# A Perceiver-style block with a mixture of experts on one core: one shared stage of the FFN moved from the front to the back, router and ranks ahead in TensorE's order, and later loads for the second block

## What is computed

```python
x = x + xattn(layernorm(x), ctx, ctx, w_proj, b_proj)      # 16 heads, softmax over 2048 keys
x = x + gated_scan_layer(layernorm(x), ...)                # tanh / sigmoid, scan over 128 rows, residual
x = x + ffn(layernorm(x), ...)

def ffn(xt):                                               # 512 tokens, 8 experts, top 2, 2 shared halves
    scores = softmax(xt @ gate_w.T); idx = top_k(scores + gate_bias, 2); weights = scores at idx
    for e in range(8):
        y += gate_e[:, None] * ((silu(xt @ w1[e].T) * (xt @ w3[e].T)) @ w2[e].T)
    z = (silu(xt @ sw1.T) * (xt @ sw3.T)) @ sw2.T          # inner width 1024: two halves of 512
    return y + z
```

## Time and profile before

| | |
|---|---|
| time, median of 3 runs | 541.11 us (536.25 to 542.07) |
| profiled execution, its run | 539.15 us |
| its span | 537.4 us |
| TensorE busy | 473.2 us (88%) |
| VectorE busy | 399.5 us (74%) |
| ScalarE busy | 330.2 us (61%) |
| GpSimd busy | 294.3 us (55%) |
| moved by DMA | 133.94 MB, mean 249 GB/s |

### The profile page before, as it was taken

How to read it: one execution, slowest core, us unless ns; L and a number is a source line. 1 busy time by engine, 2 the same in 40 slices (tenths; PEclk the granted TensorE clock), 3 DMA queues, 4 the chain that set the end, 5 groups by cost and what they waited for, 6 DMA issues and landing times.

```text
span 537.4 us, 15768 instructions
## 1 busy us (share of the span) xinstructions
PE 473.2 (88%) x6731; PEld 331.4 (62%) x6731; DVE 399.5 (74%) x603; ACT 330.2 (61%) x360; POOL 294.3 (55%) x278
## 2 busy tenths in 40 slices
PE   0579999798999898999989946997999999999995
PEld 0136667565666676666766533843788788887642
DVE  2686777477677677878762798788679999999426
ACT  3255867477567668776563463556478898887320
POOL 2358899699699999899769420472001011010032
PEclk9999999899899999999999995999999999999999
DMA  7798997959878879976696740228999999997135
GB/s 251 164 286 250 262 265 207 273 115 256 246 219 226 198 230 254 265 199 174 166 396 272 283 149 7 79 106 311 414 347 387 417 419 416 417 418 329 40 84 171
DMA packets 48249, 133.94 MB, mean 249 GB/s; under 512 B 6450, under 2 KB 31282, under 8 KB 37426
## 3 DMA queue, kind: packets, MB, share of 16 engines
q1 hardware_dynamic: 44500, 120.88, 69.6%
q0 software_dynamic: 3680, 12.06, 6.1%
HBM read 96.74 MB, written 11.01 MB: 201 GB/s over the span
## 4 chain that ended last, share of the span: by engine, by line
PE 45%; DVE 34%; issue 8%; DMA 7%; POOL 3%; ACT 1%; SPq 1%; DVEq 0%; ACTq 0%; POOLq 0%
DVE mx L696 12%; DVE ws L770 9%; PE bank L979 9%; PE bank L1014 8%; PE bank L1023 7%; PE bank L999 6%; DMA wst<-in_ffw 3%; DVE rden L713 2%; POOL xs_rows L660 2%; PE bank L1137 2%; PE bank L1139 2%; PE bank L1138 2%; DMA kt<-in_keysT 1%; DVE hf L908 1%; DMA x_tok<-xs_rows 1%
## 5 line engine op out<-in xcount | busy, mean ns | idle before, releaser
L696 DVE TENSOR_REDUCE mx<-bank 128x1 f32<-128x512 f32 x256 | 163.0, 685 | 67.9 <-PE bank L979 67.1
L457 ACT ACTIVATE pt<-bank 128x1024 f32<-128x1024 f32 x128 | 126.0, 1023 | 70.1 <-PE bank L999 70.1
L614 POOL TENSOR_TENSOR ps<-pt 128x512 f32<-128x512 f32 x128 | 160.0, 1277 | 10.1 <-ACT pt L457 5.2
L770 DVE SCALAR_TENSOR_TENSOR ws<-wst,ws 128x2048 f16<-128x2048 f32 x51 | 116.3, 2301 | 3.8 <-ACT ws L501 3.8
L979 PE MATMUL bank<-kstk,q 96*128 96x512 f16 x256 | 96.2, 407 | 24.9 <-DVE mx L696 8.1
L501 ACT ACTIVATE ws<-wst 128x2048 f16<-128x2048 f32 x48 | 90.4, 1904 | 7.1 <-DMA wst<-in_ffw 6.8
L999 PEld LDWEIGHTS bank<-q,kstk 98*128 98x128 f16 x1024 | 68.9, 100 | 22.5 <-issue 4.8
L587 POOL TENSOR_TENSOR kl<-kt,kh 128x512 f16<-128x512 f32 x62 | 70.6, 1162 | 22.3 <-ACT kh L422 22.3
L999 PE MATMUL bank<-q,kstk 98*128 98x128 f16 x1024 | 81.0, 224 | 1.0 <-ACT pt L457 1.0
L1152 PE MATMUL bank<-xt,ws 128*128 128x128 f16 x480 | 81.2, 219 | 0.6 <-DVE hf L908 0.6
L1153 PE MATMUL bank<-xt,ws 128*128 128x128 f16 x480 | 81.2, 219 | 0.0
(11 more groups left out here) (161 smaller groups left out, 639.0 us busy)
## 6 DMA issues: line engine op xcount, KB each, us to landing
wst<-in_ffw SPq DMA_DIRECT2D x51, 1024.0 KB, 10.8
kt<-in_keysT SPq DMA_DIRECT2D x16, 1024.0 KB, 6.0
kstk<-kh SPq DMA_DIRECT2D x128, 128.0 KB, 3.4
v<-in_vals SPq DMA_DIRECT2D x16, 1024.0 KB, 9.2
kstk<-kl SPq DMA_DIRECT2D x64, 128.0 KB, 3.7
xs_rows<-biases SPq DMA_DIRECT2D x15, 256.0 KB, 3.0
x_tok<-xs_rows POOLq DMA_DIRECT2D x15, 256.0 KB, 8.7
ys_rows<-xn POOLq DMA_DIRECT2D x15, 256.0 KB, 6.8
```

The lines of the kernel that those rows point to most:

```text
L457: act.activation(pt[:, n % 4, :, :, :].rearrange("p j a t -> p (j a t)"), bank[:, 2 * (n % 2):2 * (n % 2) + 2, :].rearrange("p j n -> p (j ...
L614: pool.tensor_tensor(ps2[:, n % 4, :, :], pt[:, n % 4, 0, :, :], pt[:, n % 4, 1, :, :], ALU.add)\
L696: dve.tensor_reduce(mx[:, a, q:q + 1], bank[:, 4 + k % 2, :], AX.X, ALU.max).then_inc(m_taken, 1)
L770: dve.scalar_tensor_tensor(ws[:, home_of(q), 1, m, :, :].rearrange("p c n -> p (c n)"), wst[:, q % 2, m, :, :].rearrange("p c n -> p (c n) ...
```

## The change

`STAGES` now has shared (0,0) to (0,3) in front, the 15 blocks, and shared (1,0) to (1,3) behind: 4 and 4. With it the splits of the front are dealt out anew: (3,0) goes to stage 3, and block 0 has (3,1) and (3,2) as every other block. TensorE makes only half of the first quarter ahead of the router, and one half of the third quarter is left behind the ranks. VectorE makes the slot numbers ahead of the first product, and the overflow experts and gates (`place_overflow`) behind the second stage's; split (0,2) moves from ahead of the router to behind the first stage's product. SyncE waits for the second slot rows (`xg_in[1]`) instead of the scatters ahead of load (3,0). ScalarE runs a two-element `Exp` between the third layernorm's roots. All four `combine` come ahead of the last product, all four `finish` behind it.

```diff
@@ -49,9 +49,9 @@
 NV = NB - E
 
 
-STAGES = ([("shared", 0, it) for it in range(C)] + [("shared", 1, 0)] + [("block", k, 0) for k in range(NB)]
-          + [("shared", 1, it) for it in range(1, C)])
-FRONT = C + 1
+STAGES = ([("shared", 0, it) for it in range(C)] + [("block", k, 0) for k in range(NB)]
+          + [("shared", 1, it) for it in range(C)])
+FRONT = C
 STAGE_OF = {(kind, a, it): n for n, (kind, a, it) in enumerate(STAGES)}
 
 
@@ -75,8 +75,8 @@
 def splits_at(n):
     kind, k, it = STAGES[n]
     if kind == "shared":
-        return {1: [(1, 0)], 2: [(1, 1), (2, 0)], 3: [(2, 1), (1, 2), (2, 2)], 4: [(3, 0), (3, 1)]}.get(n, [])
-    return ([(seq_of_block(k + 1), m) for m in (1, 2) if 0 < k < NB - 1] + [(seq_of_block(1), 2)] * (k == 0)
+        return {1: [(1, 0)], 2: [(1, 1), (2, 0)], 3: [(2, 1), (1, 2), (2, 2), (3, 0)]}.get(n, [])
+    return ([(seq_of_block(k + 1), m) for m in (1, 2) if k < NB - 1]
             + [(seq_of_block(k + 2), 0) for _ in range(1) if k + 2 < NB])
 
 
@@ -386,7 +386,7 @@
 
         for m in range(3):
             load_w(2, m, 1)
-        sp.wait_ge(xs_in, 16 * K_TOP * B)
+        sp.wait_ge(xg_in[1], 16)
         for m in range(3):
             load_w(3, m, 3)
         for k, m in ((2, 0), (2, 2), (2, 1), (3, 0), (3, 1), (3, 2), (4, 0)):
@@ -538,6 +538,8 @@
         split_first(2)
         for b in range(B):
             root(ln3_var, b + 1, b, b + 1)
+            if b == B - 1:
+                act.activation(r1[:, 2, 0:2], eps[:, :], ACT.Exp)
             if b > 0:
                 copy_high(b - 1)
         copy_high(B - 1)
@@ -838,7 +840,6 @@
         third_norm(B - 1)
         split_tokens(B - 2)
         split_tokens(B - 1)
-        split_low(0, 2)
 
 
         dve.wait_ge(log_ready, 1)
@@ -871,7 +872,7 @@
 
             ranks = bank[:, 1, 0:B * E].rearrange("p (b e) -> p b e", b=B)
             total = bank[:, 1, B * E:(B + 1) * E]
-            limits, order = starts[:, 1:4], iota[:, 0:NV]
+            limits = starts[:, 1:4]
 
             def per_token(row):
                 return row.unsqueeze(1).broadcast_to([P, B, E])
@@ -893,6 +894,10 @@
             link(last)
             link(dve.tensor_reduce(posf[:, :, :], rk[:, 2:4, :, :], AX.X, ALU.add))
             dve.tensor_copy(posu[:, :, :], posf[:, :, :]).then_inc(pos_ready, 1)
+
+        def place_overflow():
+
+            order = iota[:, 0:NV]
             link(dve.tensor_tensor(exb[:, :, :], ex[:, 4, :].unsqueeze(1).broadcast_to([P, NV, E]),
                                    order.unsqueeze(2).broadcast_to([P, NV, E]), ALU.is_le))
             link(dve.tensor_reduce(exo[:, :], exb[:, :, :], AX.X, ALU.add))
@@ -934,12 +939,17 @@
         for n, (kind, k, it) in enumerate(STAGES):
             todo = splits_at(n)
             if n == len(STAGES) - 1:
-                combine(0)
+                for b in range(B):
+                    combine(b)
+            if n == 0:
+                place_tokens()
             gated(n)
             if n < 2:
                 hidden_low(n)
             if n == 0:
-                place_tokens()
+                split_low(0, 2)
+            if n == 1:
+                place_overflow()
             for q, m in todo[:1]:
                 split_low(q, m)
             if n >= 2:
@@ -951,10 +961,8 @@
                 slots(k + 2)
             for q, m in todo[1:]:
                 split_low(q, m)
-        for b in range(1, B):
-            combine(b)
-            finish(b - 1)
-        finish(B - 1)
+        for b in range(B):
+            finish(b)
 
 
     @blk.tensor
@@ -1125,11 +1133,11 @@
                 mm = pe.matmul(bank[:, 4 + b, :], yst[:, b * P:(b + 1) * P], wo[:, n, :], start=(n == 0), stop=(n == 1))
             mm.then_inc(scan_out, 1)
 
-        def up(n, it, tokens=slice(0, T), last=True):
+        def up(n, it, tokens=slice(0, T), last=True, parts=range(2)):
 
             part = slice(it * P, (it + 1) * P)
             home = home_of(seq_of_stage(n))
-            for m in range(2):
+            for m in parts:
                 if n >= 2:
                     pe.wait_ge(w_lo[m], seq_of_stage(n) + 1)
                 o = bank[:, (6 if n == 1 else 4) + m, tokens]
@@ -1175,7 +1183,7 @@
         pe.wait_ge(w_lo[1], 1)
         pe.wait_ge(xl_done, 2)
         pe.wait_ge(x2_done, B)
-        up(0, 0, FIRST, False)
+        up(0, 0, FIRST, False, (0,))
 
         pe.wait_ge(gw_split, 1)
         for b in range(B):
@@ -1187,9 +1195,9 @@
                 pe.matmul(o, xh[:, c, part], gwh[:, c, E:2 * E], start=False, stop=False)
                 mm = pe.matmul(o, xl[:, c, part], gwh[:, c, 0:E], start=False, stop=(c == C - 1))
         mm.then_inc(log_ready, 1)
+        up(0, 0, FIRST, False, (1,))
         up(1, 1, FIRST, False)
-        up(0, 0, SECOND)
-        up(1, 1, SECOND)
+        up(0, 0, SECOND, True, (0,))
 
         def ranks():
             pe.wait_ge(tri_done, 1)
@@ -1234,6 +1242,8 @@
             mm.then_inc(down_done, 1)
 
         ranks()
+        up(0, 0, SECOND, True, (1,))
+        up(1, 1, SECOND)
         for n, (kind, k, it) in enumerate(STAGES):
             if n < 2:
                 continue
```

## The result

| | median us | executions | ratio to before, 95% interval |
|---|---|---|---|
| before | 540.03 | 20 (533.73 to 545.23) | |
| the changed kernel | 545.88 | 20 (539.51 to 551.97) | **1.010** [1.007, 1.013] |

The changed kernel is slower by 1.0%. The medians differ by 5.85 us, a little more than the 5.4 that the prediction took for "no change".

A forecast was written before the change was run, and what follows sets the result against it. The prediction took the weight stream over the DMA engines to end the blocks. It summed +7.8 (stage at the back), -3.1 (stream's end) and -3.4 (new end) to +1.3 us, forecast 541.3 us, range 536 to 546.

The forecast's parts named there:

- the four held scatters: GpSimd's scatters issued inside VectorE splits wait for the split's end; four marked held, the last scatter ending at 362.4 us.
- A: The forecast itself: the weight stream leads and sets the end of the blocks, 538 to 544.5 us; chance 0.50.
- the engines now wait for every load: Blocks: the 3.3 us of idle transfer at 396 to 410 vanish, ScalarE waiting for staged weights in each block.
- B: Rival: the engines lead in the blocks, block 14's product before 497 us, total 537 to 539; chance 0.15.
- C: Rival: splits hold no scatters, which are done by 358 us; total 535 to 538; chance 0.10.
- D: Rival: the load queue never gets long again, DMA share below 0.97 over 400 to 480; 546 to 548; chance 0.12.
- The stream's end: Last blocks: the late load lands at 491.2 us instead of 494.3, moving the last block's product by -3.1.
- what saves it is the queue: After late load (3,2), queued transfers make good the delay: load (4,1) lands at 388.6 against 388.4, +0.2 us.
- the second products take 4.1: TensorE, after waiting for slot rows: a stage's second products take 4.1 us, between 2.6 and 4.5, at a lower clock.
- The end, +7.8 - 3.4 = +4.4: Tail: the shared stage moved to the back adds 7.8 us; combinations ahead of the last product save 3.4.
- meets the new last product within 0.1: VectorE's end: the last combination, done 1.5 us after its start, meets the new last product within 0.1 us.
- E: Rival: one more held scatter (+1.3 us) or slot rows landing after 4.2; total 542.5 to 545; chance 0.13.

The follow-up runs named there:

- a_again: The changed kernel again with no edit, for a second profile: median 543.62 us of 6, ratio 1.0136, FFN time (first `xh` copy to end) 214.1 us.
- c_splits_ahead: Changed kernel, but VectorE makes splits (1,2) and (2,2) ahead of both slot-row copies: median 544.66 us of 6, ratio 1.0111, FFN time 211.2.
- d_old_tail: Changed kernel with the old end on VectorE, combine(0) ahead of the last product, then combine and finish by turns: median 547.26 us, ratio 1.0172, FFN time 217.7.
- f: Changed kernel with SyncE's old wait, for the scatters, ahead of load (3,0): one execution, 546.85 us, FFN time 216.0.
- h: Changed kernel with no SyncE wait at all ahead of load (3,0): one execution, 550.54 us, FFN time 215.7.
- b_again: The kernel before again with no edit, for a second profile: one execution, 537.54 us, FFN time 209.3 us (first profile 209.6).
- g: Changed kernel with no VectorE splits between split (0,2) and the seventh scatter's landing: one execution, 543.72 us, FFN time 208.6.
- k: Kernel before with router, ranks, slot numbers ahead, split (0,2) and overflow table behind, early `Exp`, no SyncE wait ahead of load (3,0): median 537.08 us, ratio 0.9965.

## Why the prediction was right or wrong

Times count from the first `xh` copy; forecast, the changed kernel, a_again.

| step | forecast | after | a_again |
|---|---|---|---|
| slot numbers | 18.4 | 18.2 | 19.7 |
| last scatter ends | 34.7 | 34.4 | 35.9 |
| first slot rows land | 39.3 | 39.3 | 40.9 |
| load (3,2) issued | 47.7 | 48.7 | 49.1 |
| product of block 14 | 171.5 | 172.8 | 174.2 |
| end | 210.9 | 213.2 | 214.1 |

**What held.** The front half came out to within 0.3 us in the first profile up to the slot rows: the slot numbers, the four held scatters, the slot rows, the wait of 4.2 for 4.1. Behind it came the steps that the diff does not say: the lower clock, the late split and the late load (3,2) behind it, 5.0 to land for 5.1. (The split stands at 373.38 in its row for 373.0 in the prediction, but this profile's first copy came 0.7 earlier, so it is 1.1 late.) From 380 to 486 the DMA engines were full as forecast A says (share 1.01 at 418 GB/s), and the last blocks end with the stream.

Not as forecast is "the engines now wait for every load". ScalarE waited for staged weights 11 times for 14.4 us, where before it was 6 times for 6.8 (and in a_again 22 times for 19.3). In the first profile two of these waits, 5.2 for (3,0) and 3.7 for (4,1), come up to 62.3 and the other nine from 135.0 on. Between them the blocks follow each other every 8.4 us, at the engines' pace, with the DMA engines full beside them; only toward the end are steps 8.6 to 9.8. The changed kernel's row in the costliest groups, then its wait for (4,1):

```profile
L501 ACT ACTIVATE ws<-wst 128x2048 f16<-128x2048 f32 x48 | 90.6, 1904 | 14.7 <-DMA wst<-in_ffw 14.4
...
389.26 1.91 ACT L501 ACTIVATE ws<-wst 128x2048 f16<-128x2048 f32 x1 [3.70 <-DMA wst<-in_ffw]
```

B is refuted: block 14's `hf` came at 499.77, not before 497. C is refuted: the last scatter ended at 361.3, not by 358. D is refuted as a mechanism: the share was not below 0.97 there, 1.00 to 1.02 in every 10 us from 400 to 480.

**What failed: the sizes of two terms.**

*The stream's end, -3.1.* The product moved by -1.8 in the first profile and -0.4 in the second. The sum had it from two steps: "what saves it is the queue", +0.2 at load (4,1), and -3.3 of idle transfer. The first is the step that failed. (4,1) landed at 62.3, against 60.7 before: +1.6. From there to the landing of block 14's w3 the stream gained 4.0, more than the 3.3, so that load landed 2.4 earlier (164.2 against 166.6) and not 3.1. In c_splits_ahead, where load (3,2) goes out in time, (4,1) lands at 61.0, +0.3, the w3 at 163.1, -3.5, and the product moves by -3.2: the queue doesn't make the late load good, and without the late load the term comes out. Some of the lateness comes from "the second products take 4.1": they took 4.8, and the first transposes 1.03 instead of 0.6, so the split that frees staging came 1.1 later, counted from the first copy. Of the 1.3 missing in the first profile 0.7 is this landing. The other 0.6 is the step from landing to product: the product followed 8.6 behind the load and not 8.0. I had carried the load's gain over whole. In a_again the later rise of the clock adds 1.5 at the slot numbers.

*The end, +7.8 - 3.4 = +4.4.* The tail measured 39.9 to 40.4 against 35.1: +4.8 to +5.3. The 3.4 is there behind the last `hf`; "meets the new last product within 0.1" was the step that failed. Four combinations, 525.57 to 531.83, are 6.3 us, and they lie between the `hl` of the last stage but one and the last product, where VectorE has some 5.7 of room. The last `hf` came 8.29 behind the one before it and not 7.8, and TensorE waited 0.8 for the `hl` of the last. In the changed kernel the gathered rows were there in time, since no combination waits for them. I had asked whether the gathered rows were there, and not whether all four would fit in one gap. d_old_tail measures the new end at 3.0, not 3.4. In the first profile one more stage, the last but one, took 8.3 instead of 7.8 (its row has 6.18 of idle time, where others have 5.69), for a reason that I did not find; f, g and h have it too, a_again and c don't.

*The bound of what is measured.* In profiles the loss is 3.5 and, with b_again and a_again, 4.7 us; the medians differ by 5.9. The 1 to 2 us between are not located. The attention part, whose code is the same, varies by 8 us from profile to profile, and whether it differs on the mean between the two kernels can't be told from one or two profiles of each.

That the range held the median is luck in part. In the profiles the sum was 2.2 to 3.4 us too low, another 1 to 2 us are not located, and the median of 545.88 lies 0.12 us under the range's upper end. By its number it is outside A's own 538 to 544.5, between E and D, whose mechanisms did not happen. Of the rivals, A held the mechanism. E, one more scatter held or a slow slot read, did not happen: four were held, as forecast, and the read took 2.9. No other rival was needed, but smaller gains: both gains of the sum were the best case of their step (a queue that makes everything good, a gap that holds everything). With the two as the first profile and d_old_tail measured them (-1.8 and -3.0) the sum is +3.0 and not +1.3; the 0.5 of the stage that has no reason makes it +3.5.

## What to carry to other kernels

Work that fills the wait for a dependent transfer is worth as much as it covers of that wait, and moving it away pays only if the wait itself ends earlier by as much: here it ended 6.5 us earlier, the stage cost 7.8 at the other end, and TensorE was left with a longer wait (4.2 for 2.8). Test the parts of a bundled change one by one; this one held a gain of 0.8% (the router and ranks ahead) under a stage move that took it away. And when a wait on the queue of loads is moved, look which split of those loads stands ahead of the urgent work on VectorE, since the engine's order makes that work as late as the load.

## What the runs showed of the hardware

- An indirect scatter issued inside a VectorE split (two inputs and the output in SBUF) ends 0.83 to 0.84 us after the split and takes 1.88 to 2.55 us, against 0.96 to 1.15 for the others, in every kernel here.
- The landing of the last scatter depends on what else is in the DMA engines: GpSimd waited 2.0 us behind it when three or four of the scatters had been held, 4.4 when the last five went out at steps of 1.26 with a 1 MB load shortly ahead of them (share 0.96; g), and 5.2 and 6.2 when two more loads had gone out ahead (h and k).
- The same instructions in the same place start at either clock: it rose 7.5 us behind the first `xh` copy in one profile of the changed kernel and 13.3 in the other, and the slot numbers moved with it, 18.2 to 19.7.
- A 1 MB load into empty DMA engines (the one 12 us ahead of the first `xh` copy) took 4.8 to 5.1 us; a 256 KB read of slot rows took 2.9 to 3.1 with no load issued beside it, against 7 to 10 in the queue. The full queue moved 416 to 417 GB/s from 420 to 480 in every kernel.
